# Counting earlier groups' router choices with matmuls, and reordering the copies of stage 1

## The reference, cut to what matters

```python
x = x + conv(ln_c(x))     # self-correlation at 28 offsets, then a 1x1 convolution
t = to_tokens(x)
t = t + ffn(ln_t(t))      # mixture of 8 experts, the two best for each token

corr = [sum(pad(f)[r:h+r, c:w+c] * f, axis=1) for r, c in offsets()]   # f: unit-length features
out  = einsum('bchw,oc->bohw', concat([feature, corr]), conv_w) + conv_b

logits = xf @ Wg
scores, idx = top_k(logits, 2);  weights = softmax(scores)
for k in range(2):
    onehot = idx[:, k, None] == arange(8)
    pos  = cumsum(onehot, axis=0) - 1        # place of a token in its expert's list
    keep = pos[own expert] < capacity        # capacity 307
    ...                                      # the expert's rows are gathered, put through
                                             # W1, silu gate and W2, weighted, added back
```

## Time and profile before

| | before |
|---|---|
| three runs | 232.94, 230.23, 229.35 us |
| profiled execution | 229.77 us, span 228.0 us |
| busy: PE, DVE, ACT, POOL | 90%, 70%, 56%, 52% of the span |
| the chain that ended last | PE 71%, DVE 11%, DMA 7%, POOL 3%, ACT 3% |
| mean granted clock of PE | 0.952 |
| DMA | 29.40 MB, 129 GB/s over the span |

### The profile page before, as it was taken

The page is one execution under the profiler, slowest core; times in us unless marked ns, Lnnn a source line. Parts: engine busy times, 40 slices in busy tenths (PEclk is TensorE's granted clock), DMA queues, the critical chain, the costliest instruction groups (busy, mean ns, idle before and its releaser), DMA issues.

```text
span 228.0 us, 4487 instructions
## 1 busy us (share of the span) xinstructions
PE 205.2 (90%) x1351; PEld 188.3 (83%) x1351; DVE 160.2 (70%) x509; ACT 128.3 (56%) x320; POOL 118.7 (52%) x130
## 2 busy tenths in 40 slices
PE   7998799869858999999999999999999999999930
PEld 2786699653327999999999999999999999999920
DVE  2674989998704599598598678679778868956520
ACT  2454765374202476587578578577568658745510
POOL 5102212100077154885877787687687683185184
PEclk9999999976795899999999999999999999999995
DMA  6648375879724392494395386288278253034043
GB/s 206 183 123 236 69 204 164 188 195 294 169 73 105 69 289 66 68 286 98 43 262 132 56 252 135 52 175 212 55 139 236 69 52 31 0 36 49 0 46 42
DMA packets 28015, 29.40 MB, mean 129 GB/s; under 512 B 6915, under 2 KB 24544, under 8 KB 28000
## 3 DMA queue, kind: packets, MB, share of 16 engines
q1 hardware_dynamic: 18656, 17.28, 26.6%
q0 software_dynamic: 7680, 9.05, 23.7%
q10 hardware_dynamic: 1664, 2.88, 4.8%
HBM read 19.86 MB, written 9.35 MB: 128 GB/s over the span
## 4 chain that ended last, share of the span: by engine, by line
PE 71%; DVE 11%; DMA 7%; POOL 3%; ACT 3%; issue 2%; SPq 1%; POOLq 0%; DVEq 0%; ACTq 0%
PE low L1173 6%; PE bank L1173 5%; PE first L1157 4%; PE first L1154 4%; PE first L1150 4%; PE first L1158 4%; PE first L1151 4%; PE low L1157 4%; PE low L1158 4%; PE low L1154 4%; PE low L1151 4%; PE low L1150 4%; PE both L1173 3%; PE low L1175 2%; PE bank L1175 2%
## 5 line engine op out<-in xcount | busy, mean ns | idle before, releaser
L500 POOL DMA_INDIRECT out<-y,goal x40 | 65.9, 1648 | 36.6 <-DVE y L933 27.4
L480 POOL DMA_INDIRECT rows<-rows_dram,source x40 | 42.5, 1062 | 36.2 <-DMA rows_dram<-row 18.9
L902 DVE TENSOR_TENSOR al<-act,ah 128x308 fp32r<-128x308 f32 x64 | 30.1, 471 | 1.0
L635 ACT CAST ah<-act 128x308 fp32r<-128x308 f32 x64 | 28.3, 443 | 1.8 <-DVE act L910 1.8
L910 DVE TENSOR_TENSOR act<-low,sil 128x308 f32<-128x308 f32 x32 | 15.3, 479 | 12.8 <-ACT sil L642 12.8
L642 ACT ACTIVATE sil<-first 128x308 f32<-128x308 f32 x32 | 13.7, 428 | 16.7 <-PE first L1158 15.6
L642 ACT ACTIVATE sil<-low 128x308 f32<-128x308 f32 x32 | 13.7, 428 | 14.2 <-PE low L1158 13.3
L910 DVE TENSOR_TENSOR act<-first,sil 128x308 f32<-128x308 f32 x32 | 15.3, 479 | 8.0 <-ACT sil L642 7.2
L1150 PE MATMUL first<-xh_a,hi_a 128*128 128x308 f32 x64 | 20.1, 314 | 0.7 <-ACT xh_a L625 0.7
L1157 PE MATMUL first<-x_b,hi_b 128*128 128x308 f32 x64 | 20.1, 314 | 0.0
L1154 PE MATMUL first<-xl_a,hi_a 128*128 128x308 f32 x64 | 19.9, 312 | 0.1
(11 more groups left out here) (172 smaller groups left out, 562.3 us busy)
## 6 DMA issues: line engine op xcount, KB each, us to landing
raw_b<-w SPq DMA_DIRECT2D x12, 256.0 KB, 4.1
raw_a<-w SPq DMA_DIRECT2D x6, 512.0 KB, 5.3
raw<-w SPq DMA_DIRECT2D x6, 384.0 KB, 6.1
gram_dram<-gram SPq DMA_DIRECT2D x8, 230.0 KB, 3.2
xt<-x_tokens SPq DMA_DIRECT2D x4, 384.0 KB, 4.4
out<-xt SPq DMA_DIRECT2D x4, 384.0 KB, 5.1
rows_dram<-row SPq DMA_DIRECT2D x3, 386.0 KB, 4.3
raw_b<-w ACTq DMA_DIRECT2D x4, 256.0 KB, 4.2
```

Of the source, the lines that this page charges most:

```text
L480: G.indirect_dma_start(out=rows[b][:, t, :], out_offset=None, in_=rows_dram, in_offset=bass.IndirectOffsetOnAxis(ap=source[:, n:n + 1], ax ...
L500: nc.gpsimd.indirect_dma_start(out=out, out_offset=bass.IndirectOffsetOnAxis(ap=goal[0:m, n:n + 1], axis=0), in_=y[0:m, t, :], in_offset=N ...
L635: nc.scalar.copy(ah[:, j, lo:hi], act[n % 3][:, 0:hi - lo]).then_inc(a_hi, 1)
L902: V.tensor_tensor(al[:, j, lo:hi], act[n % 3][:, 0:hi - lo], ah[:, j, lo:hi].bitcast(F32), ALU.subtract).then_inc(a_lo, 1)
```

## The change

The masks of the choices get one buffer for each group (`onehots[g]`), and VectorE's `chosen` and `seen` are gone with their memset and semaphore. `places(g)` counts each of the 4g earlier tiles with a matmul on `ones` of its own, ahead of its wait for this group's mask. On ACT, both gram copies of group 1 and `deviation(3)` come before `take_corr(0)`, and `load_w1` of expert 0 after it; the loads of expert 1 come before `take_corr(3)`, and that before `deviation_b(2)`. The 7 filler matmuls BUSY_FIRST are gone, and `turn_corr(1)` stands between the halves of `grams(2)`. In the last group the residual and its statistics come before the choice, and `row_scales` is split in `row_shifts` and `row_gaps`. SP stores rows of group 2 before x1 of group 1.

```diff
@@ SP
             store_x1(0)
+            store_rows(2)
             store_x1(1)
-            store_rows(2)
             store_x1(2)
@@ ACT
             deviation(2)
+            take_gram(1)
+            deviation(3)
+            take_corr(0)
             load_w1(s, 0, 0)
-            take_gram(1, (0,))
-            take_corr(0)
-            deviation(3)
-            take_gram(1, (1,))
             features(2)
...
-            deviation_b(2)
-            take_corr(3)
-            normed(2)
             load_w1(s, 1, 1)
             load_w2(s, 1, 1)
+            take_corr(3)
+            deviation_b(2)
+            normed(2)
@@ DVE, choose and find_slots
-                if g >= 1:
-                    v.wait_ge(spots_ready, g)
-                V.tensor_tensor(onehot[:, :, :, :],
+                V.tensor_tensor(onehots[g][:, :, :, :],
...
-                if g + 1 < GROUPS:
-                    v.wait_ge(choice_ready, g + 1)
-                    then(V.tensor_reduce(chosen[:, :], onehot[:, :, :, :].rearrange("p t k e -> p (k e) t"),
-                                         AX_X, ALU.add))
-                    V.tensor_tensor(seen[:, g + 1, :], seen[:, g, :], chosen[:, :], ALU.add).then_inc(seen_ready, 1)
...
+                v.wait_ge(choice_ready, g + 1)
                 v.wait_ge(place_done, g + 1)
@@ DVE, the groups' order
                 if g + 1 < GROUPS:
+                    best_scores(g)
+                    choose(g)
+                    residual(g)
+                    stats_b(g)
                     find_slots(g)
-                    row_scales(g)
+                    row_shifts(g)
+                    row_gaps(g)
                 else:
-                    row_scales(g)
+                    residual(g)
+                    stats_b(g)
+                    best_scores(g)
+                    row_shifts(g)
+                    choose(g)
+                    row_gaps(g)
                     find_slots(g)
                 spots(g)
@@ PE, places
+                if g >= 1:
+                    pe.wait_ge(slot_ready, g)
+                for p in range(g):
+                    for t in range(TILES):
+                        T.matmul(o, ones[:, :],
+                                 onehots[p][:, t, :, :].rearrange("p k e -> p (k e)").unsqueeze(1).broadcast_to([P, TILES, TOPK * E]),
+                                 start=(p == 0 and t == 0), stop=False, skip_group_check=True)
                 pe.wait_ge(choice_ready, g + 1)
...
                 if g >= 1:
-                    pe.wait_ge(seen_ready, g)
-                    pe.wait_ge(slot_ready, g)
-                T.matmul(o, ones[:, :], seen[:, g, :].unsqueeze(1).broadcast_to([P, TILES, TOPK * E]),
-                         start=False, stop=True).then_inc(place_done, 1)
+                    last = T.matmul(o, before[:, :], picks, start=False, stop=True, skip_group_check=True)
+                last.then_inc(place_done, 1)
@@ PE, order
             grams(1)
-            keep_busy(BUSY_FIRST, bank[0])
             turn_corr(0)
             conv_rest(0)
             turn_f(2)
             places(0)
-            grams(2)
+            grams(2, (0,))
             turn_corr(1)
+            grams(2, (1,))
             conv_features(1)
```

More of the change, by code:

```diff
@@ L199, in metaformer_kernel @@
         top_e = sb("top_e", [P, TILES, 8], U32)
-        onehot = sb("onehot", [P, TILES, TOPK, E], BF16)
-        seen = sb("seen", [P, GROUPS, TOPK * E], BF16)
-        chosen = sb("chosen", [P, TOPK * E])
+        onehots = [sb(f"onehot{g}", [P, TILES, TOPK, E], BF16) for g in range(GROUPS)]
         place_e = sb("place_e", [P, TILES * TOPK, E])
@@ L415, in _ @@
             G.memset(ones_f[:, :], 1.0)
-            G.memset(seen[:, 0, :], 0.0)
             G.memset(conv_b[:, C + E:], 0.0).then_inc(fills, 1)
@@ L770, in stats_b, with best_scores @@
                 last.then_inc(var_b, 1)
-            def choose(g):
+            def best_scores(g):
                 for t in range(TILES):
@@ L776, in choose @@
                 then(last)
+            def choose(g):
                 for t in range(TILES):
@@ L806, in find_slots, with row_shifts @@
                 then(V.tensor_scalar(lane[:, :], slot[:, :], P - 1, None, ALU.bitwise_and))
-            def row_scales(g):
+            def row_shifts(g):
                 v.wait_ge(sqrt_b, g + 1)
@@ L813, in row_scales, with row_gaps @@
                                        in1=rstd_b[:, tiles(g)], op0=ALU.mult, op1=ALU.mult).then_inc(shift_ready, 1)
+            def row_gaps(g):
                 then(V.tensor_tensor(unit[:, :], norm[:, tiles(g)], rstd_b[:, tiles(g)], ALU.mult))
@@ L860, in _ @@
                 combine(g)
-                choose(g)
-                residual(g)
-                stats_b(g)
                 if g + 1 < GROUPS:
+                    best_scores(g)
+                    choose(g)
+                    residual(g)
+                    stats_b(g)
                     find_slots(g)
-                    row_scales(g)
-                else:
-                    row_scales(g)
+                    row_shifts(g)
+                    row_gaps(g)
+                else:
+                    residual(g)
[4 more added lines that the diff above has]
+                    row_gaps(g)
                     find_slots(g)
@@ L984, in turn_f, with grams @@
                 last.then_inc(f_turned, 1)
-            def grams(g):
+            def grams(g, halves=(0, 1)):
                 if g >= 1:
@@ L990, in grams @@
                 fa, fb = ft_a[g], ft_b[g]
-                for t in range(TILES):
+                for t in [2 * h + i for h in halves for i in range(2)]:
                     if g == 0 and t == 0:
@@ L1056, in places @@
                     pe.wait_ge(before_ready, 1)
+                o = bank[7][:, 0:TILES * TOPK * E]
+                if g >= 1:
[5 more added lines that the diff above has]
+                                 start=(p == 0 and t == 0), stop=False, skip_group_check=True)
                 pe.wait_ge(choice_ready, g + 1)
-                o = bank[7][:, 0:TILES * TOPK * E]
-                picks = onehot[:, :, :, :].rearrange("p t k e -> p (t k e)")
-                T.matmul(o, before[:, :], picks, start=True, stop=False)
+                picks = onehots[g][:, :, :, :].rearrange("p t k e -> p (t k e)")
                 for d in range(1, TILES):
                     n = d * TOPK * E
-                    T.matmul(o[:, n:], ones[:, :], picks[:, 0:TILES * TOPK * E - n], start=False, stop=False,
+                    if g == 0 and d == 1:
+                        T.matmul(o, before[:, :], picks, start=True, stop=False, skip_group_check=True)
+                    last = T.matmul(o[:, n:], ones[:, :], picks[:, 0:TILES * TOPK * E - n], start=False, stop=(g == 0 and d == TILES - 1),
                              skip_group_check=True)
                 if g >= 1:
-                    pe.wait_ge(seen_ready, g)
-                    pe.wait_ge(slot_ready, g)
-                T.matmul(o, ones[:, :], seen[:, g, :].unsqueeze(1).broadcast_to([P, TILES, TOPK * E]),
-                         start=False, stop=True).then_inc(place_done, 1)
+                    last = T.matmul(o, before[:, :], picks, start=False, stop=True, skip_group_check=True)
+                last.then_inc(place_done, 1)
             def fill_table(g):
```

8 lines of the change are left out of this document (4 added, 4 removed).

## The result

| | before | after |
|---|---|---|
| median (lowest to highest, 5 runs each) | 230.23 us (229.16 to 232.94) | 236.8 us (235.99 to 238.58) |
| profiled execution, span | 229.77, 228.0 | 236.8, 235.0 |
| mean granted clock of PE | 0.952 | 0.937 |
| P (last `part`) | 49.30 | 56.78 |
| first gather | 62.69 | 68.55 |

What follows compares the result with a forecast made beforehand. The first expert's start was taken as the bound, set by VectorE's chain to P, then the path to the gathers. Up to P 1.5 us (0.7 + 0.8), then 1.8: 3.3 off 229.77 gives 226.5 us, range 223.6 to 230.2.

Steps and rivals of the forecast that it cites:

- The loads next to the small reads: Expert 1's loads beside group 3's gram store and read: 0.5 us more for each, hidden by PE's 0.9 us slack.
- The estimate from the Trainium skill's latency figure: Group 3's store and read: 1.8 us more for each, making the forecast some 2 us worse.
- Group 1: gram copy first: Group 1's second gram copy 2.3 to 2.7 us earlier, store and read with it; worth 0.7 us, bounds 0 and 1.1.
- features(2): On ACT behind three weight issues and take_corr(0), yet 0.3 us earlier, between 0 and 0.6.
- the clock inside stage 1: Rival, chance 0.17: without the filler PE's clock falls to half for 6.2 us, losing 3.1 us; 229.6 us.
- the late `near` of group 3: Rival, chance 0.14: store and read take 3.3 us more together, VectorE waits 1.9 us for the root; 228.4 us.
- a top of 232.7: Rival slower than before, chance 0.05: two low-clock stretches, over grams(2) and over grams(3) and conv(2), twice 3.1 us.
- The low end, 223.6: Low edge of the forecast range, taking in the full 3.1 us from a first expert at full clock.
- Group 0: Without the filler, group 0's transposes and VectorE's start come 1.0 us earlier, between 0.6 and 1.3.
- Counting: VectorE drops `chosen` and `seen`, 0.39 us per group; 0.8 us from groups 1 and 2, PE's extra matmuls costed at nothing.
- The last group: New order from P to the gathers: row store issued 1.0 us earlier, landing in 3.3; gathers 1.8 us earlier, bounds 1.0 to 2.1.
- the three signs of being wrong: Clock at 0.50 between 20 and 40; group 2's `sd_b` waiting for a transpose; `source` or the store gating at P + 12.

Runs made afterwards that it cites:

- e1: Changed kernel with expert 1's loads put back behind normed(2); ratio to the kernel before 1.0174.
- e3: Kernel before with only expert 1's loads moved ahead of deviation_b(2); ratio to the kernel before 1.0052.
- e8: e1 with expert 0's w1 loads ahead of group 1's gram copies again; ratio to the kernel before 1.0154.
- e9: e1 with the 7 filler matmuls ahead of group 0's transposes put back; ratio to the kernel before 1.0164.
- e6: Kernel before with only the counting by matmuls; ratio to the kernel before 1.0043.
- f1: Changed kernel with the last group's steps back in the old order; ratio to the kernel before 1.0241.
- e10: e6 with expert 1's loads moved behind normed(3) on ACT; ratio to the kernel before 1.0267.
- f2: e6 with expert 1's loads issued by SP right behind the last row stores; ratio to the kernel before 0.9997.
- e2: Changed kernel with deviation_b(2) ahead of take_corr(3) on ACT again, loads still early; ratio to the kernel before 1.0335.
- f3: e5 with expert 1's loads issued by SP right behind the last row stores; no ratio, median of 4 runs 239.93 us.
- f4: Kernel before with only expert 1's loads issued by SP right behind the last row stores; ratio to the kernel before 1.0067.
- g1: The kernel of f3 once more, on another chip; ratio to the kernel before 1.0011.
- g2: The kernel of f2 once more, beside g1 on the same chip; ratio to the kernel before 1.0005.
- e4: Kernel before with counting by matmuls and the last group's new order; ratio to the kernel before 1.0146.
- e5: e4 with 4 instead of 14 filler matmuls ahead of the last table fill; no ratio, median of 4 runs 230.99 us.
- e7: e1 with group 1's transposes behind all of grams(2) again; ratio to the kernel before 1.0138.
- e12: Kernel before with only expert 1's loads moved behind normed(3) on ACT; ratio to the kernel before 1.0077.

## Why the prediction was wrong, step by step

- **The loads next to the small reads** is the step that failed. I took 0.5 us each for store and read, hidden by 0.9 of slack. Together they grew by 5.8 us (5.58 to 11.37), 4.7 of it by the loads (e1 has 6.67), and VectorE waited 5.08 us for the root behind them; without the loads P comes 5.73 us earlier (e1). I had read landing times of single DMAs and never asked how many bytes would stand ahead: the four loads are 2 x 256, 512 and 384 KB (the page's DMA issues), 1.44 MB. At the 237 GB/s of 39 to 51 us that is 6.1 us, at the 270 of its last part 5.3: an estimate somewhat above the 4.7 measured here and well above the 3.5 of e3, but of the right size. The Trainium skill's rule ("DMA: Bandwidth & Descriptors", "Issuing engines are not separate DMA queues") that ACT's queue does not spare SP's is what the trace shows: SP's store and read took 6.01 and 5.18 us beside loads from ACT's queue. The estimate from the Trainium skill's latency figure, some 2 us worse, was nearer than mine and still under half.
- **Group 1: gram copy first.** The copy moved by 2.8 us as said (18.41), its store and read did not: `near` reached POOL 0.83 us earlier (26.73). Copy to POOL is 7.86 us instead of 5.91; expert 0's loads were issued in it, from 19.35 (e8, with those loads in front, has 7.19, its store 5.62 of that). I counted their wait on ACT, not their bytes. I had `part` of group 1 at 31.4; it came at 34.16.
- **features(2)** I had 0.3 us earlier, and it was: PE's `turn_f(2)` at 23.30, before 23.55. But PE had started 1.1 earlier, so its gap grew to 1.65 us. The clock fell 4.5 us later; with a gap of 0.18 (e8) it did not.
- **Rivals.** Two happened, the clock inside stage 1 (0.17) and the late `near` of group 3 (0.14, sized at 1.9 us of wait, 5.08 measured). I had given the missing filler as the reason of the first, and e9 shows that it is not. I had set them side by side as exclusive, with a top of 232.7; they add, and both come from weight loads moved into stage 1. Even added at my prices (3.1 and 1.9 us) they give 231.5: the sizes were wrong too. The low end, 223.6, is 0.2 above the 223.4 that 226.5 - 3.1 gives; it changes nothing.
- **Group 0** (1.0 us) was right: 1.08.
- **Counting** (0.8 us) looks right and was luck: e6 has P 0.75 us earlier, but only 0.28 of it is VectorE's in groups 1 and 2. I had taken PE's counts as covered, and in group 1 VectorE waits 0.28 us for them. A gain of 0.28 us is 0.1% of the time and less than its runs can tell; why the interval (1.0000 to 1.0086) leans to slower stays open.
- **The last group** (1.8 us to the gathers): P to gathers went from 13.39 to 11.77, 1.62 won. The last row store was issued at P + 6.9, as forecast, and landed in 3.4 us, where I had 3.3. But f1 gives 0.67 of it to the order, and only 0.92 reached the transposes. e3, without the order, has 1.09, so what counts there is that the loads had left. The fillers ahead of the table were a step that I left out; `source` came 1.03 us later relative to P, not 0.1.

Of the signs I had named, `turn_corr(0)` at 18.66, the gram copy, ACT's last rows (P + 4.3) and the row store's issue and landing held. All that hung on `near` did not, and two of the three signs of being wrong came: the clock at 0.50 at 28 us, and `sd_b` of group 2 behind a copy that waits for transposes.

## What to carry to other kernels

Before moving a bulk load, find the small store-and-read chains in the stretch that it enters, and price them by the bytes that will stand ahead of them (MB over the GB/s of that stretch), not by the spread of landing times. Here that gave 5.3 to 6.1 us where 4.7 and 3.5 were measured, so it was an upper figure. Rivals with one cause are added, not weighed against each other. When a step moves on one engine, look at which fillers were placed by its old time.

## What the hardware did that I had not expected

- DMAs written behind activations on ACT were issued beside them: e10's loads at 54.05, as the first of `normed(3)`'s rows only began. The kernel before shows it too: the loads behind `normed(2)` go out at 47.16, its first row starts at 47.15. That a DMA stands in ACT's order says when it is issued, and not that the activations ahead of it are done. To hold a transfer back, its place in SP's order worked (f2), its place in ACT's did not.
- The last row store lands in 3.2 to 3.4 us with the last load issued 19 us or more ahead of it (after, e2, e3, f1), 3.6 to 3.8 with the loads issued right behind it (f2, f3, f4, g1, g2), 3.91 and 4.47 with the last load issued 8.3 us ahead (e6, before), 5.2 to 5.95 with 7.2 to 7.7 us between them (e1, e4, e5, e7, e8, e9), 7.31 to 7.61 with the loads right in front (e10 to e12).
- In the five traces in which `source` ends last (after, e2, e4, f3, g1) the second gather takes 1.28 or 1.29 us on POOL, in the fifteen others 0.96. VectorE splits weights at that time; whether that is the cause was not tried.
